# Top-2 expert layer on one core: the lower rows of five tiles scaled by ScalarE and added by GpSimd, of three by VectorE

## What is computed

```
xt = x @ W.T + b + (x @ A[adapter]) @ B[adapter] * 2           # the conditioning layer
scores = softmax(xt @ router_w + router_b) + router_bias        # 16 experts in 4 groups
idx = the best 2 experts of the best 2 groups;  gate = scores[idx]
y = sum over the 2 chosen e of  gate[e] * ((silu(xt@w1[e]+b1[e]) * (xt@w2[e]+b2[e])) @ w3[e] + b3[e])
z = (silu(xt@sw1+sb1) * (xt@sw2+sb2)) @ sw3 + sb3               # the shared expert
out = x + y + z
```

## Time and profile before

| | |
|---|---|
| three runs | 158.26, 159.47, 160.37 us; median 159.47 |
| the profiled execution's own time | 158.81 us |
| its span in the trace | 157.0 us (1.8 us lie outside of it) |
| granted TensorE clock | full speed throughout |
| PE busy | 146.0 us, 93% of the span |
| DVE busy | 95.4 us, 61% |
| ACT busy | 52.5 us, 33% |
| POOL busy | 52.2 us, 33% |
| DMA | 43.1 MB, 275 GB/s on average |

### The profile page before, as it was taken

One profiled execution on the slowest core, in us unless ns is written; L12 is line 12 of the kernel. 1 busy time (PEld: TensorE's weight loads), 2 busy tenths in 40 slices (PEclk: granted clock), 3 DMA queues, 4 the chain that ended last, 5 costly groups with the idle time before them and its releaser, 6 DMA issues.

```text
span 157.0 us, 2751 instructions
## 1 busy us (share of the span) xinstructions
PE 146.0 (93%) x828; PEld 109.9 (70%) x829; DVE 95.4 (61%) x243; ACT 52.5 (33%) x110; POOL 52.2 (33%) x69
## 2 busy tenths in 40 slices
PE   3979999999989999999889999999999998799991
PEld 3857676776857777898676677777776775378760
DVE  1762475188787679979614556654533453368993
ACT  3462152542722261145164333433343332400000
POOL 7720220000000020427225575777566656330000
PEclk9999999999999999999999999999999999999999
DMA  4999978999977699999442456787776799935994
GB/s 147 375 262 361 398 267 262 363 411 414 414 250 289 174 380 357 391 454 336 129 125 69 136 192 209 221 279 256 249 223 244 162 347 342 293 138 187 320 380 182
DMA packets 16669, 43.14 MB, mean 275 GB/s; under 512 B 2224, under 2 KB 2224, under 8 KB 16400
## 3 DMA queue, kind: packets, MB, share of 16 engines
q1 hardware_dynamic: 11392, 25.41, 45.8%
q0 software_dynamic: 3776, 12.59, 25.2%
q10 hardware_dynamic: 1488, 4.98, 8.3%
HBM read 34.06 MB, written 8.91 MB: 274 GB/s over the span
## 4 chain that ended last, share of the span: by engine, by line
PE 69%; DVE 12%; DMA 8%; ACT 5%; issue 3%; SPq 1%; DVEq 0%
PE bank L983 22%; PE bank L1158 20%; PE bank L1176 9%; PE bank L1148 5%; DMA condW_raw<-in_condWT 4%; DMA xg_sb<-xt_rows,slot_tok 4%; DVE x_sb L934 4%; DVE x_sb L947 3%; PE bank L1046 3%; PE bank L1026 2%; DVE x_sb L942 2%; PE bank L1169 2%; PE bank L1036 1%; PE bank L1003 1%; PE bank L1138 1%
## 5 line engine op out<-in xcount | busy, mean ns | idle before, releaser
L1158 PE MATMUL bank<-w_sb,xgT_sb 128*128 x144 | 37.0, 382 | 0.8 <-issue 0.7
L1158 PEld LDWEIGHTS bank<-w_sb,xgT_sb 128*128 128x128 f32 x144 | 25.4, 190 | 11.8 <-issue 9.1
L457 POOL DMA_INDIRECT xg_sb<-xt_rows,slot_tok x22 | 21.3, 968 | 15.6 <-PE bank L1148 6.2
L463 POOL DMA_INDIRECT y_rows<-y_ring,slot_row x18 | 19.6, 1087 | 17.8 <-DVE y_ring L876 17.8
L864 DVE TENSOR_TENSOR pre_sb<-bank,b_sb 128x256 f32<-128x256 f32 x18 | 7.6, 424 | 24.2 <-PE bank L1158 21.9
L1176 PE MATMUL bank<-w_sb,hT_sb 128*128 x36 | 18.5, 595 | 0.6 <-ACT hT_sb L607 0.6
L983 PE MATMUL bank<-condW_h,xT_h 128*128 128x512 f32 x32 | 14.2, 442 | 0.8 <-DVE condW_l L676 0.8
L876 DVE COPY y_ring<-bank 128x512 f32<-128x512 f32 x18 | 12.3, 684 | 1.5 <-issue 1.5
L983 PE MATMUL bank<-xtT_h,sw_h 128*128 128x512 f32 x32 | 13.2, 412 | 0.0
L983 PE MATMUL bank<-condW_l,xT_h 128*128 128x512 f32 x32 | 12.8, 400 | 0.0
L599 ACT COPY xgT_sb<-bank 128x512 f32<-128x512 f32 x18 | 10.6, 587 | 6.5 <-PE bank L1148 5.5
(11 more groups left out here) (168 smaller groups left out, 253.7 us busy)
## 6 DMA issues: line engine op xcount, KB each, us to landing
w_sb<-in_w SPq DMA_DIRECT2D x8, 1024.0 KB, 10.4
w_sb<-in_w ACTq DMA_DIRECT2D x2, 2048.0 KB, 16.1
xt_rows<-xt_ring SPq DMA_DIRECT2D x8, 256.0 KB, 5.0
b_sb<-in_b SPq DMA_DIRECT2D x1, 2048.0 KB
x_sb<-in_x SPq DMA_DIRECT2D x8, 256.0 KB
low_sb<-y_rows SPq DMA_DIRECT2D x4, 512.0 KB
high_sb<-y_rows SPq DMA_DIRECT2D x4, 512.0 KB, 5.6
out<-x_sb SPq DMA_DIRECT2D x8, 256.0 KB, 3.0
```

What stands on the lines that cost most here:

```text
L457: pool.indirect_dma_start(xg_sb[:, b % 4, :], None, xt_rows, bass.IndirectOffsetOnAxis(ap=slot_tok[:, b:b + 1], axis=0)).then_inc(gathered ...
L463: pool.indirect_dma_start(y_rows, bass.IndirectOffsetOnAxis(ap=slot_row[:, b:b + 1], axis=0), y_place(b), None).then_inc(y_scattered[b % Y ...
L1158: mm = pe.matmul(bank[2 + s % 2][:, 0:2 * INTER], xgT_sb[:, s % 2, k, :], w12_sb[:, bass.ds(e * W12 + k * 2 * INTER, 2 * INTER)], start=(k ...
```

## The change

The set of tiles whose lower rows DVE doesn't add grows from (5, 6, 7) to (3, 4, 5, 6, 7), and it is done in another way: ACT multiplies these tiles of `low_sb` by the gates, in place, once all lower rows are in; GpSimd, after its last scatter, adds them to x in `x_sb`. The diagonals and PE's three matmuls with them are gone. DVE's order is another one, and it waits for GpSimd (`low_added`) before it touches a tile of the five. ACT and GpSimd load `low_at` into a register ahead of the loop, PE no longer does.

```
-LOW_ON_PE = (5, 6, 7)
+LOW_ON_POOL = (3, 4, 5, 6, 7)
...
-        diag = at(48, "diag", [P, len(LOW_ON_PE), P])
...
@@ gpsimd
             top = last_group(pool)
+            pool.wait_ge(low_known, 1)
+            first = low_at(pool)
...
+            pool.wait_ge(x_in, 16 * TILES)
+            for n, i in enumerate(LOW_ON_POOL):
+                pool.wait_ge(low_scaled, n + 1)
+                pool.tensor_tensor(x_sb[:, i, :], x_sb[:, i, :], low_tiles(first, i), ALU.add).then_inc(low_added, 1)
@@ scalar
             left = blocks_left(act)
+            act.wait_ge(low_known, 1)
+            first = low_at(act)
...
-            for n, i in enumerate(LOW_ON_PE):
-                act.activation(diag[:, n, :], ident[:], ACT.Copy, scale=val[:, 0, i:i + 1]).then_inc(diag_ready, 1)
+            act.wait_ge(low_in, 16 * TILES // 2)
+            for i in LOW_ON_POOL:
+                act.activation(low_tiles(first, i), low_tiles(first, i), ACT.Copy, scale=val[:, 0, i:i + 1]).then_inc(low_scaled, 1)
@@ vector
             def add_shared(i, last=False):
+                if i in LOW_ON_POOL:
+                    dve.wait_ge(low_added, LOW_ON_POOL.index(i) + 1)
                 dve.wait_ge(shared_done, i + 1)
...
             def add_high(i, last=True):
                 dve.wait_ge(high_in[i // 2], 16)
+                if not last:
+                    dve.wait_ge(low_added, LOW_ON_POOL.index(i) + 1)
...
             dve.wait_ge(low_in, 16 * TILES // 2)
-            add_low(0)
-            add_shared(0)
-            add_low(1)
-            add_low(2)
-            add_shared(1)
-            add_low(3)
-            add_shared(2)
-            add_low(4)
+            for i in range(3):
+                add_low(i)
+                add_shared(i)
             add_shared(3)
+            add_shared(4)
             add_high(0)
             add_high(1)
-            add_shared(4)
+            add_shared(5)
             add_high(2)
             add_high(3)
-            add_shared(5)
+            add_shared(6)
             add_high(4)
             add_high(5)
-            add_high(6, last=False)
-            add_shared(6, last=True)
+            add_high(6)
             add_high(7, last=False)
             add_shared(7, last=True)
@@ tensor
-                if b == 2:
-                    pe.wait_ge(low_known, 1)
-                    first = low_at(pe)
...
-                mm = pe.matmul(shared_bank(i)[:], gateT[:, i * P:(i + 1) * P], b3s_split[:], start=False,
-                               stop=(i not in LOW_ON_PE))
-                if i in LOW_ON_PE:
-                    n = LOW_ON_PE.index(i)
-                    pe.wait_ge(diag_ready, n + 1)
-                    pe.wait_ge(low_in, 16 * TILES // 2)
-                    mm = pe.matmul(shared_bank(i)[:], diag[:, n, :], low_tiles(first, i), start=False, stop=True)
-                mm.then_inc(shared_done, 1)
+                pe.matmul(shared_bank(i)[:], gateT[:, i * P:(i + 1) * P], b3s_split[:], start=False, stop=True
+                          ).then_inc(shared_done, 1)
```

More of the change, by code:

```diff
@@ L248, in program @@
         shared_done, acc_shared = sem("shared_done"), sem("acc_shared")
-        diag_ready = sem("diag_ready")
+        low_scaled, low_added = sem("low_scaled"), sem("low_added")
         low_in = sem("low_in")
```

## The result

The changed kernel takes 162.22 us (median of 4 runs, 162.03 to 162.65), the kernel before 158.87 us in the same comparison (4 runs, 157.31 to 160.37). The ratio is 1.025, with a 95% interval of 1.020 to 1.031: slower by about 4 us. I had forecast 159.8 us and no change; the time lies above my range (158.5 to 161.3), near its rival 1 at the upper end.

The account below looks back on a forecast made before the run. The tail was bound by DVE's 21 instructions, then one store, with PE close behind. Terms 0.1 + 0.3 - 0.1 = +0.3 us gave 159.1 against the profiled execution, 159.8 us against the median; range 158.5 to 161.3.

Parts of the forecast that it names:

- rival 1: Tail: GpSimd's sums hold DVE up, 161.0 us at 1.3 us of work each, 163.2 at 1.76; chance 0.19, 0.06 over 2%.
- PE's part: Tail: three diagonals go, banks open 1.63 us apart, the last bank comes 2.5 us earlier, the first five as before.
- DVE's part: Tail: two add_low fewer, but DVE idles before banks 3 and 4 instead; bank 4 holds the end, +0.1 us.
- ScalarE's part: Tail: five products of 128x512 replace three of 128x128, each ahead of the sum that waits for it; costs nothing.
- GpSimd's part: Tail: five sums, 1.0 us of work each, fit mostly into DVE's idle time, DVE getting in between them; +0.3 us.
- the sum's second term: Tail: the delay of DVE by GpSimd's five sums, taken as +0.3 us in the forecast's total.
- My bound: Tail: at most +3.8 us, if each GpSimd sum holds DVE off for 1.76 us.
- my own placement: Tail: GpSimd's five sums laid out from 140.3 to 146.7 between DVE's instructions, ahead of add_high(0) at 147.1.
- three signs of being wrong: Tail: GpSimd still adds after 148, add_high takes over 0.8 us each, or DVE has no gap before bank 4.
- Registers: Expert loop's steps: PE's dropped load of low_at gives -0.1 us; ACT's added load is covered by 0.47 us.
- Rival 3: Loop: ACT's added register load reaches PE and costs 0.3 us, the last store as late, 160.4 us; chance 0.06.

## Why the prediction failed, step by step

- **PE's part: right.** Without diagonals PE's last matmul runs from 150.65 to 151.05, where I had about 151.1; banks open 1.63 us apart.
- **DVE's part: right.** +0.1 us forecast, +0.08 measured without the sums, with the two gaps where I had put them.
- **ScalarE's part: right.** The five products took 3.18 us from 136.93, each done before the sum that needed it.
- **GpSimd's part: the step that failed.** The price of one sum was nearly right: I took 1.0 us of work and 0.1 to 0.2 between two; they run at 1.25 us. What was wrong is that I let DVE in after each one ("the first works 140.3 to 141.3 and pushes `add_low(1)` from 140.66 to 141.3"). In the changed kernel DVE got in after none of them: `add_low(1)` was done at 146.75, 0.55 us behind the fifth sum. The row I reasoned from the earlier trace rows showed one GpSimd sum between two DVE instructions; it could not show how the turn passes inside a run of sums, and I didn't name that as unknown. The 0.3 us of the sum's second term measured 3.55 us. The Trainium skill's rule (SBUF — State Buffer, Who interferes with whom) speaks of one instruction waiting for the whole of the other. The trace agrees where DVE waited for one sum (1.22 us for `add_low(1)` with both loads late), and goes beyond it in the changed kernel: there DVE waited for five.
- **My bound came near by luck.** +3.8 us came from 1.76 us of work for each sum, five times 0.76 us over the 1.0 I took. The sums were not that long; they were not parted. The prices of rival 1 don't follow from my own placement either: a fifth sum that ends at 148.3 is 1.2 us behind the 147.1 at which `add_high(0)` wants its turn, not 1.6.
- **The signs.** Of the three signs of being wrong, one came: DVE has no gap before bank 4. GpSimd was done at 146.20, and four `add_high` took 2.74 us together.
- **Registers: wrong in sign.** I had -0.1 us. From the first to the fourth `turn_h` PE took 91.47 - 81.53 = 9.94 us before (the fourth is in the earlier trace rows, the first below), 91.51 - 80.99 = 10.52 in the changed kernel and 9.77 with ScalarE's load late. So PE's load less gives 0.17, and ScalarE's load more costs 0.75: 0.53 in the first step (4.04 against 3.51) and 0.22 in the second, whose cause I don't know. All profiles agree: 10.51 to 10.59 us in the eight with ScalarE's load ahead, 9.77 to 9.81 in the four without it, 9.90 and 9.94 in the two with PE's. These are the two rows of the kernel before that the earlier trace rows doesn't show, and ACT's and PE's rows of the changed kernel:

```profile
81.53 0.30 PE L1169 MATMUL bank<-ident,h_sb 128*128 128x128 f32 x1 [0.53 <-DVE h_sb L869]
...
84.11 1.13 PE L1158 MATMUL bank<-w_sb,xgT_sb 128*128 x4
```

```profile
80.43 0.60 ACT L587 CAST hsT_h<-hsT_sb 128x512 fp32r<-128x512 f32 x1
82.23 0.27 ACT L613 COPY hT_sb<-bank 128x128 f32<-128x128 f32 x1 [1.20 <-PE bank L1177]
...
82.64 1.12 PE L1184 MATMUL bank<-w_sb,hT_sb 128*128 x2
84.07 1.13 PE L1166 MATMUL bank<-w_sb,xgT_sb 128*128 x4 [0.31 <-issue]
```

I had taken the time from the copy's end (82.50) to PE's use of it (82.97) as cover. But PE waits for that copy at the head of a queue: behind the matmul stand two register loads (`last_group` and the next block's expert), which can't begin before it. In both kernels the copy ends at 82.50 and the matmuls behind the loads start 1.6 us later, at 84.11 and 84.07. There was no cover. The load was also longer than the 0.33 us that I had taken as its most: from the cast's end to the copy it is 81.57 to 82.23 before, 0.66 us, and 81.03 to 82.23 with the third load, 1.20 us, so 0.54 for the third. The wait for `low_known` in front of it is not that time: VectorE's instruction that counts it ended at 77.1. Rival 3's mechanism was right, and larger than I priced it.

The sum as measured is 0.08 + 3.55 + 0.58 = 4.2 us, within the interval of the ratio (3.2 to 4.9 us). The spans differ by 3.6, since the changed kernel's profiled execution reached the loop 0.54 us sooner (80.99 against 81.53).

**What stays open.** Why a run queued 0.7 us or more before a scatter's end keeps DVE out, and the same run queued later does not; the runs show when it happens and not by what. I didn't try a run behind another kind of GpSimd instruction.

## What to carry to other kernels

When work moves from VectorE to GpSimd, look at each VectorE instruction that runs beside it: one with two inputs in SBUF may wait for the whole run of GpSimd's, one with an input in PSUM didn't wait here. Put the two-input work ahead of the run, or part the run from the scatter before it by one wait, and look for the cost in the length of instructions, since the list of waits did not show it. And what stands behind a wait in an engine's program, register loads too, starts only after it (here the matmuls behind PE's loads came 1.6 us after the copy, whenever PE used the copy): a producer has no slack just because its matmul comes a little later.

## What the runs showed of the hardware that I had not expected

- A GpSimd sum of 128x512 float32 takes 1.25 us in a run, and five of them, queued behind a scatter, held a two-input VectorE instruction for 5.4 us; three held it for 3.0 us.
- A pause of 0.24 us behind one sum let VectorE in, and after a memset of one column (0.11 us) with a wait, VectorE came in between sums that follow without a pause.
- A GpSimd sum that was queued 0.2 us after VectorE had asked still went first, while the run lasted (one profile).
- The same five sums held VectorE for one at a time when the first was queued 0.2 us before the scatter's end or later, and for all five when it was queued 0.7 us before it.
- One more register load on ScalarE, ahead of the loop's first copy, cost 0.75 us of the loop's first three steps.
